# Key-stacking transfers moved from SyncE's queue to ScalarE's, with a new order of all stages

## What is computed

```python
q = heads(hidden_states @ W_q)
k_t = heads(text_ehs @ W_k)
v_t = heads(text_ehs @ W_v)
scores_t = jnp.einsum('bhsd,bhtd->bhst', q, k_t) * attn_scale
probs_t = jax.nn.softmax(scores_t, axis=-1)
text_out = jnp.einsum('bhst,bhtd->bhsd', probs_t, v_t)
...
attn_scores = jnp.einsum('bhsd,bhnd->bhsn', q, k_ip) * attn_scale
qsem = _l2norm(jnp.einsum('bhst,bte->bhse', probs_t, text_ehs))
sem = jnp.einsum('bhse,bne->bhsn', qsem, ip_n)
probs_ip = jax.nn.softmax(attn_scores + SEM_SCALE * sem, axis=-1)
...
out = (text_out + ip_out) @ W_out + b_out + residual
```

## Time and profile before

| what | value |
|---|---|
| three runs | 445.45, 442.94, 445.0 us; median 445.0 |
| the profiled execution | 443.75 us, of which 441.9 us lie between first and last instruction |
| mean granted TensorE clock | 0.985 of full speed |
| busy | PE 90%, VectorE 66%, ScalarE 50%, GpSimd 44% |
| chain that ended last | PE 25%, VectorE 25%, GpSimd 15%, DMA 14%, SP queue 8%, issue 8%, ScalarE 4% |
| key-stacking transfers | 96 from SP, 80 KB each, median 2.8 us from issue to landing |
| query-stacking transfers | 96 from SP, 160 KB each, median 5.0 us |

### The profile page before, as it was taken

The page is one execution under the profiler, slowest core; times in us unless marked ns, Lnnn a source line. Parts: engine busy times, 40 slices in busy tenths (PEclk is TensorE's granted clock), DMA queues, the critical chain, the costliest instruction groups (busy, mean ns, idle before and its releaser), DMA issues.

```text
span 441.9 us, 13510 instructions
## 1 busy us (share of the span) xinstructions
PE 397.1 (90%) x5172; PEld 240.4 (54%) x5172; DVE 292.1 (66%) x817; ACT 221.2 (50%) x489; POOL 192.8 (44%) x480
## 2 busy tenths in 40 slices
PE   6996979899999999999899867989999899998985
PEld 3454444555655665556555534554666566555643
DVE  3334827776778777967887774776776667666723
ACT  2341414554645545454455443456776676565651
POOL 5030303566666765656567648474442352211000
PEclk9898989999999999999999999899999999999999
DMA  8575371603606125052052037252652734637052
GB/s 210 130 102 112 85 90 27 115 4 98 90 12 117 17 68 74 4 116 48 6 114 26 3 54 88 67 78 65 74 118 52 110 83 56 115 63 102 4 168 74
DMA packets 27881, 33.57 MB, mean 76 GB/s; under 512 B 5733, under 2 KB 17193, under 8 KB 27817
## 3 DMA queue, kind: packets, MB, share of 16 engines
q1 hardware_dynamic: 26949, 31.31, 39.9%
q10 hardware_dynamic: 868, 1.39, 1.1%
HBM read 5.82 MB, written 2.62 MB: 19 GB/s over the span
## 4 chain that ended last, share of the span: by engine, by line
PE 25%; DVE 25%; POOL 15%; DMA 14%; SPq 8%; issue 8%; ACT 4%; DVEq 0%; POOLq 0%
DVE mx L1189 9%; PE ps L676 8%; POOL e L1342 7%; DVE wt L1156 6%; DMA qs<-qp 6%; DMA qs<-mt 4%; SPq L660 4%; PE ps L753 4%; PE ps L783 3%; SPq L651 3%; PE ps L859 2%; DMA wt<-in_WKIP 2%; POOL e L1349 2%; PE ps L825 2%; DMA ks<-kp 2%
## 5 line engine op out<-in xcount | busy, mean ns | idle before, releaser
L1085 ACT ACTIVATE pt<-ps 128x512 f32<-128x512 f32 x160 | 88.4, 595 | 69.3 <-PE ps L783 68.7
L1189 DVE TENSOR_REDUCE mx<-ps 128x8 f32<-128x480 f32 (+3 forms) x192 | 105.1, 578 | 11.2 <-PE ps L753 11.1
L825 PE MATMUL ps<-pt,gram 64*32 64x256 f32 x1280 | 86.5, 387 | 1.6 <-ACT pt L1085 1.5
L831 PE MATMUL ps<-pt,vb 64*32 64x256 f32 x640 | 85.6, 388 | 0.0
L802 PE MATMUL ps<-wt,cst 64*32 64x256 f32 x640 | 85.3, 388 | 0.0
L532 POOL TENSOR_TENSOR qp<-qr,qp 80x512 bf16<-80x512 f32 x28 | 32.4, 1157 | 77.3 <-ACT qp L1068 77.3
L753 PE MATMUL ps<-ks,qs 96*128 96x128 bf16 x640 | 54.8, 223 | 8.4 <-DMA ks<-kp 2.9
L783 PE MATMUL ps<-qs,ks 101*128 101x256 bf16 x320 | 52.4, 276 | 8.3 <-DMA qs<-mt 5.2
L1156 DVE TENSOR_TENSOR wt<-ps,pt 128x512 f32<-128x512 f32 x80 | 54.5, 681 | 4.9 <-PE ps L825 4.9
L753 PEld LDWEIGHTS ps<-ks,qs 96*128 96x128 bf16 x640 | 40.8, 99 | 30.4 <-issue 12.2
L1145 DVE TENSOR_TENSOR qr<-ps,qp 80x512 f32<-80x512 f32 x32 | 21.8, 683 | 41.7 <-ACT qp L1064 41.5
(11 more groups left out here) (112 smaller groups left out, 708.6 us busy)
## 6 DMA issues: line engine op xcount, KB each, us to landing
qs<-qp SPq DMA_DIRECT2D x96, 160.0 KB, 5.0
ks<-kp SPq DMA_DIRECT2D x96, 80.0 KB, 2.8
xa<-in_xT SPq DMA_DIRECT2D x8, 160.0 KB, 2.7
out_T<-xa SPq DMA_DIRECT2D x7, 160.0 KB, 2.2
ca<-in_ctxT ACTq DMA_DIRECT2D x2, 512.0 KB, 7.2
xa<-in_xT SPq DMA_DIRECT2D x8, 96.0 KB, 3.0
out_T<-xa SPq DMA_DIRECT2D x7, 96.0 KB, 2.3
qs<-mt SPq DMA_DIRECT2D x32, 20.0 KB
```

Source lines behind the costliest of these rows:

```text
L825: last = nc.tensor.matmul(ps[T * hh + 32 * m:T * hh + 32 * m + 32, bank, sub * S:(sub + 1) * S], gram[keys_of(hh), g % V_RING, 32 * m:32 * ...
L831: nc.tensor.matmul(region(pair, hh), stationary(g, pair, keys_of(hh)), pt[keys_of(hh), (5 * g + c) % P_RING, sub, :], start=(c in (0, 3)), ...
L1085: nc.scalar.activation(pt[:, (5 * g + c) % P_RING, :, :].rearrange("p a b -> p (a b)"), ps[:, 2 + (g + c) % 2, :], ACT.Exp, scale=SCALE).t ...
L1189: nc.vector.tensor_reduce(mx[:, tile, p0:p0 + np_, :], o[:, :, :, 0:nt], AX_X, ALU.max).then_inc(red_done, 1)
```

## The change

`stack_keys` leaves SP and becomes three stages of ScalarE, `kd` 0, 1 and 2, one for each part: three, two and one transfers. They wait for the same semaphores as before, on ScalarE. The two loads of the constant rows of layer 1's keys, which `stack_keys` also issued, stay on SP as a stage `kr1` of their own. All offset tables, `MOVED` and the bank tables have new numbers, so the order of the stages changes on every engine.

```diff
@@ ACT_AT
+    ("kd", 0): (-1.78, 3.2095), ("kd", 1): (-1.4251, -1.5236), ("kd", 2): (-4.3234, -3.7686),
...
@@ SP_AT
-    ("xd", 0): (-8.844, None), ("qd", 0): (-2.1487, 9.8514), ("kd", 0): (-1.5649, 9.7377),
+    ("xd", 0): (-13.6043, None), ("qd", 0): (-12.9356, 0.2697), ("kr1", 0): (None, 3.6205),
...
@@ runs
+    if what == "kr1":
+        return g in (B, B + 2)
...
@@ block.sync
-            def stack_keys(g, _):
-
+            def second_rows(g, _):
 
                 slot = g // 2 % 2
-                need(sp, st_ps, 5 * (g // 2 * 2 - 2))
-                if g in (B, B + 2):
-                    static_rows(1, slot, 1, rows1_in[slot])
-                for part, made in enumerate((k_h, k_m, k_l)):
-                    sp.wait_ge(made, g // 2 + 1)
-                    for j in [j for j, p in enumerate(K_PARTS) if p == part]:
-                        sp.dma_start(ks[16 * j:16 * j + 16, slot, :, :, :], kp[:, slot, part]).then_inc(k_stacked[slot], 16)
+                sp.wait_ge(st_ps, 5 * (g // 2 * 2 - 2))
+                static_rows(1, slot, 1, rows1_in[slot])
...
@@ block.scalar
+            def stack_keys(g, part):
+
+                slot = g // 2 % 2
+                if part == 0:
+                    need(act, st_ps, 5 * (g // 2 * 2 - 2))
+                act.wait_ge((k_h, k_m, k_l)[part], g // 2 + 1)
+                for j in [j for j, p in enumerate(K_PARTS) if p == part]:
+                    act.dma_start(ks[16 * j:16 * j + 16, slot, :, :, :], kp[:, slot, part]).then_inc(k_stacked[slot], 16)
```

More of the change, by code:

```diff
@@ L145 @@
-DVE_AT = {
[L146 to L156, removed]
[12 rows of a table added]
@@ new lines @@
+    ("yr", 0): (0.1261, -0.9156), ("warm", 0): (-1.0102, None), ("warm", 1): (-1.3287, None),
+    ("warm", 2): (-0.3338, None), ("warm", 3): (-3.6613, None), ("warm", 4): (-0.4112, None),
+    ("warm", 5): (-0.3879, None)}
+ACT_AT = {
+    ("kd", 0): (-1.78, 3.2095), ("kd", 1): (-1.4251, -1.5236), ("kd", 2): (-4.3234, -3.7686),
+    ("kh", 0): (-4.3234, -4.6404), ("qh", 0): (-3.0679, -3.2226), ("km", 0): (-3.7281, -3.8079),
+    ("qm", 0): (-2.8984, -2.7726), ("setup", 0): (-0.9607, None), ("iplen", 0): (1.2156, None),
+    ("keys1", 0): (-4.3154, None), ("keys1", 1): (-4.0082, None), ("mtev", 0): (-0.4805, -0.3024),
+    ("gram", 0): (0.7237, None), ("gram", 1): (-1.4765, None), ("gram", 2): (-0.2574, None),
+    ("gram", 3): (-0.9399, None), ("gram", 4): (0.0129, None), ("gram", 5): (-1.3292, None),
+    ("exp", 0): (0.0641, 0.4542), ("exp", 1): (0.0094, -1.7626), ("exp", 2): (-0.9911, -1.4933),
+    ("exp", 3): (0.3499, -3.843), ("exp", 4): (-0.0385, -3.7766), ("otev1", 0): (1.0517, 1.2947),
+    ("otev2", 0): (1.2013, 1.3802), ("stat", 0): (1.4588, None), ("stat", 1): (1.2116, None),
+    ("rsq", 0): (1.5615, None), ("ipe", 0): (2.2691, None), ("ztev", 0): (2.6841, 2.5526),
+    ("ztev2", 0): (None, -2.7233)}
@@ new lines @@
+DVE_AT = {
+    ("kmask", 0): (-0.8166, -0.643), ("kr", 0): (3.0299, -1.6048), ("setup", 0): (-6.8732, None),
+    ("qr", 0): (-3.3548, -3.2671), ("kl", 0): (-3.4986, -1.3245), ("ql", 0): (-0.03, -0.8031),
+    ("red", 0): (-1.0613, -0.7657), ("red", 1): (-0.957, -0.8409), ("red", 2): (-4.3388, -0.7372),
+    ("red", 3): (-0.8206, -0.771), ("red", 4): (-2.8388, -1.1521), ("neg", 0): (-0.6157, -0.5308),
+    ("vprep", 0): (-3.2101, None), ("vprep", 1): (0.713, None), ("vprep", 2): (0.5624, None),
+    ("vprep", 3): (0.9977, None), ("vprep", 4): (2.4115, None), ("vprep", 5): (-0.997, None),
+    ("vprep", 6): (2.8827, None), ("vprep", 7): (2.4978, None), ("vprep", 8): (-2.7128, None),
+    ("vprep", 9): (4.7146, None), ("w", 0): (-0.026, None), ("w", 1): (0.1298, None), ("w", 2): (0.3894, None),
+    ("w", 3): (0.5237, None), ("w", 4): (0.6345, None), ("on", 0): (1.5018, 1.6629), ("on", 1): (1.5597, -4.4463),
+    ("ipa", 0): (1.5319, None), ("wz", 0): (1.8867, None), ("ipm", 0): (1.9401, None), ("ipr", 0): (2.3695, None),
+    ("ysb", 0): (2.649, -3.2128), ("ysb2", 0): (None, -0.2617), ("yrsb", 0): (-0.62, -2.6035)}
@@ new lines @@
+    "POOL": {("ipd", 0, 0): 2.2811, ("ipz", 0, 0): 2.7738, ("ipd", 0, 1): 2.6362, ("vpb", 0, 1): 1.1968,
+        ("ipb", 0, 2): 2.0212, ("ipz", 0, 2): 2.8594, ("ipz", 0, 3): 2.8882, ("vpb", 0, 3): 1.3359,
+        ("ipd", 0, 4): 2.2772, ("vpb", 0, 4): -2.604, ("ipb", 0, 5): 2.1541, ("ipz", 0, 5): 2.9967,
+        ("ipb", 0, 6): 2.1861, ("kmask", 0, 6): -3.9164, ("vpb", 0, 7): 0.9176, ("ipb", 0, 8): 2.1193,
+        ("kl", 0, 8): -2.5909, ("kmask", 0, 8): -4.001, ("vpb", 0, 8): 1.5693, ("ipb", 0, 10): 1.9336,
+        ("ipz", 0, 10): 2.6909, ("kl", 0, 10): -2.8364, ("ql", 0, 10): -2.2178, ("ipb", 0, 11): 1.8034,
+        ("ipz", 0, 11): 2.8588, ("ipb", 0, 12): 2.0633, ("ipb", 0, 13): 2.0275, ("ipd", 0, 13): 2.0943,
+        ("ipz", 0, 14): 2.6693, ("kl", 0, 14): -3.0984, ("kmask", 0, 14): -3.9292, ("kr", 0, 14): -3.8105,
+        ("ipb", 0, 15): 1.7333, ("ql", 0, 15): -2.529, ("vpb", 0, 15): 1.6289, ("kmask", 0, 16): -4.6764,
[7 rows of a table added]
@@ new lines @@
+    "SP": {("late0", 0, 0): 2.051, ("mtd", 0, 0): -0.3769, ("mtd", 0, 1): 0.1651, ("mtd", 0, 2): 0.4688,
[4 rows of a table added]
+        ("mtd", 0, 16): 12.628, ("mtd", 0, 17): 13.8408, ("outd", 0, 17): 32.2597, ("mtd", 0, 18): 4.0207,
+        ("mtd", 0, 19): 12.3763, ("qd", 0, 19): 9.8436, ("mtd", 0, 21): 11.4473, ("qd", 0, 21): 9.9017,
+        ("mtd", 0, 23): 12.3972, ("outd", 0, 23): 37.4968, ("outr", 0, 23): 34.6443, ("qd", 0, 23): 8.6403,
+        ("mtd", 0, 25): 10.9507, ("qd", 0, 25): 7.9568, ("mtd", 0, 27): 11.9464, ("qd", 0, 27): 8.838,
+        ("mtd", 0, 28): 7.5612, ("mtd", 0, 29): 12.9101, ("outr", 0, 29): 33.8465, ("qd", 0, 29): 9.0679,
+        ("outd2", 0, 31): 38.6795, ("qd", 0, 31): 10.6291}}
@@ L665, in stack_maxima @@
                 sp.dma_start(qs[KR:KR + MR, slot, :, b2 * S:(b2 + 1) * S], mt[:, b2, :]).then_inc(m_stacked[b2], 16)
-            run("SP", {"mtd": stack_maxima, "late0": load_late, "late1": load_layer1, "xd": load_x, "outd": store, "outd2": store2, "outr": store_rest, "kd": stack_keys, "qd": stack_queries})
+            run("SP", {"mtd": stack_maxima, "late0": load_late, "late1": load_layer1, "xd": load_x, "outd": store, "outd2": store2, "outr": store_rest, "kr1": second_rows, "qd": stack_queries})
             sp.wait_ge(out_done, 16 * (2 * (B // 2 + 2) + 8))
```

134 lines of the change are left out of this document (70 added, 64 removed), and 204 rows, old and new, of tables (BANK_MOVED, FILL_BANK, MOVED, PE_AT).

## The result

The changed kernel took 467.39 us, the median of three runs (467.33 to 468.22), against 445.0 before: a ratio of 1.053 (95% interval 1.049 to 1.057), so slower by about 22 us. The forecast was 440.8 us with a range to 450.0. It was wrong.

A forecast was written before the change was run, and what follows sets the result against it. TensorE was taken as the bound, busy 397.1 of 441.9 us. Terms -2.9 - 0.8 + 1.0 - 2.4 + 1.6 + 0 - 0.7 = -4.2 gave 439.55 us, or 440.8 us against the 445.0 median; range 434.0 to 450.0.

The forecast's parts named there:

- The step that failed: Layer 1: key groups on ScalarE use some 24 of its 40.4 idle us, so they cost nothing.
- My own term of -2.4 for the maxima: Layer 1: maxima transfers with no key issues ahead in SP's queue save 2.4 us, bounds 0 and -3.0.
- Shared engines: Rival, no change: both queues use the same DMA engines, keys and queries still collide; 445.9 us, chance 0.18.
- my signs of a wrong prediction: Layer 0 odd steps over 0.8 us longer, ScalarE issues near 1 us or more, or queries landing later among interleaved keys.
- The clock was a term in one place only: Change of layers: without the long stop, part of the granted clock's loss returns, -0.8 us, bounds 0 and -1.8.
- Start: First two blocks: keys are stacked later but PE waits for queries there; 0 us, bounds -4 and +2.
- Change of layers: Around step 16: key wait gone -2.9, clock -0.8, later maxima eviction at step 17 +1.0; -2.7 us.
- +4.9 for ScalarE: Layer 0, seven odd steps: a key group ahead of the zt eviction delays the query cast, 0.7 us a block.
- -3.3 for the order: Layer 0: the new order wins back a third of PE's 9.8 idle us.
- ScalarE late: Rival, slower: key groups on ScalarE stand ahead of what PE needs next; 449.8 us, chance 0.19.
- The price of an issue, 0.62 us: ScalarE: SP's 0.595 us per key transfer scaled by the WQ ratio 1.04; 59 us for 96 issues.
- End: End of kernel: two transposes of z move ahead of the last value products; -0.7 us, bounds 0 and -1.5.

The follow-up runs named there:

- Run 1: Changed kernel with key transfers of half the size from the third block on, same number of transfers and issues; 448.2 us, ratio 1.007.
- run 6: Changed kernel with the key transfers of steps 0 and 2 issued by SP again at their old places; 461.1 us, ratio 1.034.
- run 5: Changed kernel with keys of steps 20 to 30 on SP again, ahead of the maxima of step g-2, and step 30's `kl` earlier; 450.16 us, ratio 1.010.
- run 7: Changed kernel with the six key issues of steps 20 to 30 in one piece on ScalarE, ahead of the query burst; 466.28 and 468.79 us.
- run 9: Changed kernel with ScalarE's keys of steps 20 to 30 split, three issues behind the copy of zt, three behind the maxima's eviction; 458.86 us, ratio 1.032.
- run 10: New order of the other engines, all keys on SP, step 16's keys ahead of step 15's maxima, step 30's `kl` earlier; 438.68 us, ratio 0.988.
- run 11: Changed kernel with only the keys of steps 4 to 18 on ScalarE, the others on SP, step 30's `kl` earlier; 444.93 us, ratio 1.004.
- run 4: Kernel before with the keys of step 16 ahead of the maxima of step 15 in SP's queue; 442.2 us, ratio 0.994.
- run 3: Kernel before, its order kept, with keys of steps 4 to 30 issued by ScalarE, six in one piece; 482.27 us, ratio 1.082.
- run 8: Kernel before with step 16's keys ahead of step 15's maxima and layer 1's keys behind the maxima of step g-2, all on SP; 470.41 us, ratio 1.055.

## Why the prediction was wrong

**The step that failed** is "The key groups on ScalarE cost nothing here by this sum: they go into its 40.4 idle us". I looked for the cost of a key group only on ScalarE and never asked when its bytes would be on the DMA engines. What came was +20.3 us, since the groups ran beside the query bursts. Its parts are as follows. Run 1 gives the bytes' share, 125.04 - 108.44 = 16.6 us (12.0 against run 6). Run 1 alone does not tell coinciding from sheer load; but where the groups stand apart from the bursts with all their bytes (runs 5, 7, 9, 10 and 11) they land in 2.8 us, and where SP issues them (5, 10 and 11) layer 1 takes 107.8 to 109.1. The new order with keys on SP takes 107.79 (run 10), so 108.44 - 107.79 = 0.65 is left for ScalarE being held by its issues where the change puts them, no more than layer 1 differs between runs 5 and 11 with the same lists (109.1 and 107.8). The order itself costs 107.79 - 104.74 = 3.05, or 2.0 against run 4. Why the order costs that was not tried. My own term of -2.4 for the maxima did not come: they were issued at once, as forecast, and PE waited 11.0 us for them.

**The rival that named the cause was mispriced.** Shared engines was there, with the right evidence, and I let it only keep an old wait, at 445.9 us. I dismissed it by the mean DMA share, 0.32 and 0.48. A mean over a stretch says nothing on two bursts that start within 0.6 us of each other. The query burst alone held SP for 3.8 us in the kernel before and for 5.2 after. Whether layer 1's groups would start beside it was to be asked by laying the new lists over the times of before, which I did for step 16 alone. "Query transfers landing later because the keys now interleave with them" stood among my signs of a wrong prediction, without a price.

**The clock was a term in one place only.** I priced it at the change of layers and not for the case that new waits come. In layer 1 it made up 8.1 of 16.6 us, and 4.0 of 12.0 in run 6. I also took PE's idle time, 44.8 us, for all that an order can change; its busy time rose by 10.3.

**Start: 0 became +7.0**, outside its bounds of -4 and +2. "Queries are what PE waits for there" held for the first scores before, 1.2 us, though maxima cost more, 3.3. After, the first keys were issued from 23.69 in place of 17.23, together with the queries, and took 8.9 us (median) to land. Run 11, with these keys back on SP, reaches the mark 6.3 us earlier, at 73.79; of these 3.8 are PE's idle time (18.56 and 14.74).

**Change of layers: right, but for the clock.** Predicted -2.7, measured -3.96; run 4 shows the early keys alone to be worth 2.8 us in the medians. PE's idle time there fell by 3.4 us (8.96 to 5.61). The granted clock was 0.97 before and after, so the 0.8 us that I expected of it did not come in the profiled execution. The new order adds more: run 10 takes 61.1 us there against 66.8 in run 4, of which 2.6 are busy time at a clock of 1.00 in place of 0.97.

**Layer 0: right in sum, not in its parts.** Predicted +4.9 for ScalarE and -3.3 for the order. Measured, the order gives +0.8 (run 10 less before) and the keys +1.6 (run 11 less run 10), some 0.3 us a block; the keys' part takes in SP's own list too, which also differs between the two. The order did win idle time, but lost it again. PE in layer 0, before, after and in run 10:

```profile
73.05:246.49 173.44, 162.42 (x2792) 98.73 (x2800) 134.18 (x406) 87.00 (x207) 110.92 (x319) 1.00 0.33 59
80.08:256.24 176.16, 166.26 (x2792) 98.64 (x2800) 135.22 (x405) 88.05 (x208) 112.94 (x320) 1.00 0.35 61
72.24:246.47 174.23, 165.41 (x2792) 98.78 (x2800) 134.81 (x405) 88.24 (x208) 112.65 (x320) 1.00 0.35 59
```

Idle time falls from 11.02 us to 8.82 in run 10, 2.2 of my 3.3, and is 9.90 in the changed kernel. But the same 2792 matmuls are busy for 3.0 and 3.8 us longer, at an unchanged clock. I had no term for that, and why it is so stays open.

**ScalarE late: right in kind, wrong in place.** Where the change puts the groups it costs 3 to 4 us in all by the profiled executions: 1.6 in layer 0, 1.3 at the change of layers (runs 11 and 10, 62.4 and 61.1) and 0.65 in layer 1. The medians of runs 11 and 10 lie 6.3 us apart (444.93 and 438.68), and run 11's profiled execution was its fastest, so the cost may be larger. It is a large cost elsewhere: run 3 loses 19.1 us in layer 0 with six issues in one piece. The price of an issue, 0.62 us from a ratio of two other rows, came as forecast:

```profile
L1230 ACTq DMA_DIRECT2D ks<-kp x96: 567/616/1949, 23.7 to 425.9; - x96
```

**End: right in sign**, -1.59 for -0.7, just past its bound of -1.5.

The rule of the Trainium skill that I made a rival (DMA: Bandwidth & Descriptors, Issuing engines are not separate DMA queues) agrees with all runs: a second issuing engine bought only issue time on SP, which SP had to spare. The runs show a cost beside that: the packets' own time grew by a seventh here.

## What to carry to other kernels

When a DMA group moves to another queue, lay the issue times of both queues side by side and ask which bursts now overlap and which small urgent transfer follows them; the mean DMA share does not answer that. One in-order queue is also a regulator, and a stage that it works off while it would wait for the urgent one is free there, while the same stage behind the urgent one cost 30 us in layer 1 (runs 8 and 4). Look first for a move inside the list that exists: one line of SP's order was worth 2.8 us, and with a better order of the engines 5.
